# Summing the states of a selective scan by accumulating transfers, and sending token numbers instead of token rows

## The chip, the cores and the metric

One core of one Trainium2 chip. The metric is device microseconds of one execution of the whole program, all of it float32; the profile is of one further execution. PE is the matrix engine (PEld its weight loads), DVE the vector engine, ACT the scalar engine, POOL the GpSimd engine and SP the engine that issues most transfers. A queue of transfers carries the name of the engine that issues it (SPq, POOLq).

## What is computed

Three blocks with a residual each, on 16 sequences of 64 tokens of 512 numbers (1024 tokens):

```python
x = x + xattn(layernorm(x), ctx, ctx)        # 16 heads of 64: the reshape makes one row of 16 heads out of two
                                             # rows of 512, so 32 query rows and 256 key rows a sequence
x = x + ssm(layernorm(x))                    # d_inner 1024, 16 states
x = x + moe(layernorm(x))                    # 16 experts, 4 of them a token, hidden width 256

# inside ssm, for each token t of a sequence:
h = exp(dt[:, :, None] * A) * h + dt[:, :, None] * B_t * x_t[:, :, None]
y_t = einsum('bds,bs->bd', h, C_t) + D * x_t          # a sum over the 16 states s
# then y @ out_proj_w.T
```

In the mixture each token's rank over the experts gives it four slots, each expert's slots are cut in blocks of 128 rows, and the four expert outputs of a token are added with its weights.

## The kernel before

The 16 sequences go in four groups (0 to 3) of 256 tokens. A group passes attention, then projections, then the scan of its 16 states; the loop over groups runs the attention of group g+1 beside the scan of group g. Order on each engine is written out by hand and semaphores tie the engines together.

**The scan** (`scan_step`, DVE). Each state of a group is three DVE instructions over 128 x 2048: the input `u*B` into `state` (L1347), the scan itself with the decay (L1350), and the product with C (L1354) which is written over the decay buffer it has just used. ACT writes the decays, eight activations a state (L1104, `scan_decay`). There are three decay buffers (NDEC), so the decay of state j+3 may be written only when the product of state j has been read; ACT waits for that in `decay_buffer_free`. The B and C rows come broadcast from DRAM by SP into two buffers (`load_bc`, tile `bc_bcast`).

**The sum over states**, groups 0 to 2. PE adds in PSUM: `start_sum` (L673) multiplies `D*x` by the identity into four banks, and `sum_state` (L679) adds one product, four matmuls of 128x512, each of which the profile shows as two records. So a state is 8 records. They stand in PE's program between the matmuls of the next group's attention: states 0 to 2 in `attn_prep`, 3 to 11 in the eight attention units, 12 and 13 at the attention's end, 14 and 15 in `projections`. `copy_sum` brings the banks back. Group 3's states are added on DVE (L1361) beside the first experts.

**Attention.** `attn_prep(g)` makes the queries (L616), a bias of the keys (L622), and the queries carried into the context's space (L646), copied out by ACT (L959), with one decay after each of four pieces. `key_bias` (ACT, L980, eight activations) and `row_bias` (PE, L665, 16 matmuls of one column) turn the key bias into one number a row; `neg_max` on DVE (L1289, L1290) uses it. A unit then is scores (L691), exponentials, transposes (L700) and the weighted context (L712). After eight units come L743 and L751, and DVE adds the result to the residual (L1296). SP loads 1 MB of context a unit (`ctx`), and after each attention 4 MB of projection weights (`queries_ctx<-in_dt_t` first), which PE needs at L772.

**The experts.** POOL clears the table of slots in DRAM (`xd`, 20,224 rows of 2 KB), 40 transfers of up to 1 MB (L1632), one allowed after each of the attention units 8 to 15 in turns. For each group it then scatters token rows into the slots by 32 indirect transfers (`dispatch`, L1641). SP loads 128 rows a block (`load_block_x`, L453); there are 39 blocks of groups 0 to 2 and 23 of group 3 (wave 1). A block is a transpose (L801), gate and up (L811), a transpose of the hidden row (L820) and down (L832). POOL gathers outputs by 32 indirect transfers (`collect`, L1650).

## Time and profile before

| | us |
|---|---|
| three timed runs | 1369.01, 1369.88, 1376.7 (median 1369.88) |
| profiled execution, its own time | 1377.52 |
| span of its trace | 1375.8 |
| PE busy | 1176.5 (86%) |
| DVE busy | 881.7 (64%) |
| ACT busy | 631.7 (46%) |
| POOL busy | 134.1 (10%) |
| HBM read, written | 197.03 MB, 68.29 MB |

A busy share is a mean over stages with different limits. A row of the timeline has start and duration in us, then engine, line, operation, output<-input, and in brackets how long the engine was idle before it and who ended that. "128*128" of a matmul is the weight tile; a count of records of PE is twice that of its matmuls. A line number is one of the kernel before.

### The profile page before, as it was taken

What the parts mean: (1) busy time and instruction counts of PE and PEld (TensorE: products, weight loads), DVE (VectorE), ACT (ScalarE), POOL (GpSimd) and SP (SyncE); (2) the same over time, 40 slices, a digit from 0 to 9 for tenths busy, and PEclk for the clock granted to TensorE, in tenths of its full rate; (3) what the DMA queues carried; (4) which work ended last, traced back from release to release, by engine and by line L of the source; (5) the groups of instructions that cost most, each with busy time, mean ns of one, the idle gap of its engine ahead of it and who ended that gap; (6) DMA issues with size and microseconds to landing.
All of it is one profiled execution on the core that took longest, in us unless ns stands there. A gap on an engine that the chain in (4) does not pass through costs nothing.

```text
span 1375.8 us, 13572 instructions
## 1 busy us (share of the span) xinstructions
PE 1176.5 (86%) x4404; PEld 757.3 (55%) x4404; DVE 881.7 (64%) x946; ACT 631.7 (46%) x1398; POOL 134.1 (10%) x113
## 2 busy tenths in 40 slices
PE   5996869777897899999789999935999999999993
PEld 4884736555464557667456766533454445545451
DVE  1121376875657789995878998585999993323312
ACT  4452565445247466736555663642545441223221
POOL 0010001311000007000001600021000000223102
PEclk9897988999899799999889999957999998999997
DMA  7256101999630025540003523018899993999993
GB/s 272 77 169 251 40 16 43 388 401 358 213 127 8 9 70 160 150 144 15 14 10 107 168 60 140 9 61 297 317 380 358 363 374 111 371 354 408 409 397 123
DMA packets 114037, 266.22 MB, mean 194 GB/s; under 512 B 10160, under 2 KB 43056, under 8 KB 113968
## 3 DMA queue, kind: packets, MB, share of 16 engines
q1 hardware_dynamic: 98096, 207.16, 43.2%
q0 software_dynamic: 15872, 58.20, 10.8%
q8 instruction: 36, 0.59, 0.2%
q14 instruction: 33, 0.27, 0.1%
HBM read 197.03 MB, written 68.29 MB: 193 GB/s over the span
## 4 chain that ended last, share of the span: by engine, by line
PE 50%; DVE 29%; DMA 9%; ACT 8%; issue 3%; POOL 1%; SPq 0%; POOLq 0%; DVEq 0%; ACTq 0%
DVE state L1350 10%; PE bank L811 8%; PE bank L679 7%; PE bank L772 7%; PE bank L691 5%; DVE state L1347 5%; PE bank L832 4%; PE bank L712 4%; DMA ctx<-in_ctx_t 4%; DVE state L1357 2%; DVE y_acc L1361 2%; DVE decay L1354 2%; ACT decay L1104 2%; PE bank L616 2%; PE bank L646 2%
## 5 line engine op out<-in xcount | busy, mean ns | idle before, releaser
L1350 DVE TENSOR_TENSOR_SCAN state<-decay,state 128x2048 f32<-128x2048 f32 x64 | 283.0, 4421 | 40.2 <-ACT decay L1104 39.4
L811 PE MATMUL bank<-expert_w,block_x_t 128*128 128x512 f32 x496 | 227.4, 602 | 1.8 <-ACT block_x_t L1156 1.7
L679 PE MATMUL bank<-decay,params 128*128 128x512 f32 x384 | 183.5, 624 | 4.3 <-DVE decay L1354 4.3
L1104 ACT ACTIVATE decay<-delta_even,params 128x256 f32<-128x256 f32 x256 | 107.2, 496 | 103.7 <-PE bank L679 95.2
L1641 POOL DMA_INDIRECT dispatched<-ffn_x,slot x32 | 73.0, 2281 | 779.0 <-DVE slot L1443 770.5
L811 PEld LDWEIGHTS bank<-expert_w,block_x_t 128*128 128x128 f32 x496 | 91.8, 195 | 93.9 <-issue 91.9
L691 PE MATMUL bank<-ctx,queries_ctx 128*128 128x256 f32 x512 | 120.8, 392 | 19.7 <-DMA ctx<-in_ctx_t 18.5
L712 PE MATMUL bank<-probs,ctx 128*128 128x256 f32 x512 | 121.9, 393 | 11.6 <-ACT probs L1013 6.9
L1104 ACT ACTIVATE decay<-delta_odd,params 128x256 f32<-128x256 f32 x256 | 106.2, 499 | 43.6 <-PE bank L679 34.0
L679 PEld LDWEIGHTS bank<-decay,params 128*128 128x128 f32 x384 | 75.5, 200 | 84.7 <-issue 78.0
L712 PEld LDWEIGHTS bank<-probs,ctx 128*128 128x128 f32 x512 | 100.9, 198 | 36.4 <-issue 14.9
L832 PE MATMUL bank<-expert_w,hidden_t 128*128 128x512 f32 x248 | 117.0, 594 | 2.9 <-ACT hidden_t L1170 2.9
L772 PE MATMUL bank<-normed_t,queries_ctx 128*128 128x256 f32 x512 | 115.0, 385 | 4.2 <-DMA queries_ctx<-in_dt_t 3.1
L691 PEld LDWEIGHTS bank<-ctx,queries_ctx 128*128 128x128 f32 x512 | 98.5, 197 | 36.5 <-DMA ctx<-in_ctx_t 19.9
L1498 DVE SCALAR_TENSOR_TENSOR hidden<-hidden,bank 128x256 f32<-128x256 f32 x62 | 26.1, 421 | 142.2 <-ACT hidden L1160 129.0
L772 PEld LDWEIGHTS bank<-normed_t,queries_ctx 128*128 128x128 f32 x512 | 98.5, 193 | 22.9 <-issue 4.1
L1354 DVE TENSOR_TENSOR decay<-state,bc_bcast 128x2048 f32<-128x2048 f32 x48 | 109.5, 2282 | 0.8
L1347 DVE TENSOR_TENSOR state<-u_even,bc_bcast 128x2048 f32<-128x2048 f32 x32 | 73.4, 2293 | 37.4 <-DMA bc_bcast<-bc_scratch 36.6
L1160 ACT ACTIVATE hidden<-bank 128x256 f32<-128x256 f32 x62 | 23.7, 382 | 141.8 <-PE bank L811 133.4
L832 PEld LDWEIGHTS bank<-expert_w,hidden_t 128*128 128x128 f32 x248 | 46.8, 190 | 61.1 <-issue 57.4
L1166 ACT ACTIVATE block_y<-bank 128x512 f32<-128x512 f32 x62 | 37.1, 598 | 83.6 <-PE bank L832 79.0
L1347 DVE TENSOR_TENSOR state<-u_odd,bc_bcast 128x2048 f32<-128x2048 f32 x32 | 73.3, 2290 | 0.8
(196 smaller groups left out, 1398.9 us busy)
## 6 DMA issues: line engine op xcount, KB each, us to landing
dispatched<-ffn_x POOLq DMA_DIRECT2D x38, 1024.0 KB, 25.0
expert_w<-in_eg_t SPq DMA_DIRECT2D x62, 512.0 KB
expert_w<-in_eu_t SPq DMA_DIRECT2D x62, 512.0 KB
expert_w<-in_ed_t SPq DMA_DIRECT2D x62, 512.0 KB, 9.7
ctx<-in_ctx_t SPq DMA_DIRECT2D x32, 512.0 KB, 6.9
ctx<-in_ctx_n SPq DMA_DIRECT2D x32, 512.0 KB, 4.3
bc_bcast<-bc_scratch SPq DMA_DIRECT2D x64, 256.0 KB, 6.0
block_x<-dispatched SPq DMA_DIRECT2D x62, 256.0 KB
```

Of the source, the lines that this page charges most:

```text
L679: mm = pe.matmul(y_bank[c][:, :], ident, dA[(g * NS + j) % NDEC][:, c * 512:(c + 1) * 512], start=False, stop=(j == NS - 1))
L691: mm = pe.matmul(o, QT[g][:, k, c, qb * P:(qb + 1) * P], ctxT[n % 2][:, c, :], start=(c == 0), stop=(c == DC - 1))
L712: mm = pe.matmul(b[:, cc * Q:(cc + 1) * Q], ctxN[n % 2][:, j, c * P:(c + 1) * P], probT[n % 2][:, j, :], start=(j == 0), stop=(j == KC - 1))
L772: mm = pe.matmul(b[:, kk * gt:(kk + 1) * gt], w[:, c, (k + kk) * P:(k + kk + 1) * P], xT[g][:, c, :], start=(c == 0), stop=(c == DC - 1))
L811: mm = pe.matmul(o, xbT[q % 2][:, c, :], w_gu[q % NW][:, :, c, :], start=(c == 0), stop=(c == DC - 1))
L832: mm = pe.matmul(bank[4 + q % 2][:, :], hidT[q % 2][:, c, :], w_dn[q % NW][:, c, :], start=(c == 0), stop=(c == IC - 1))
L1104: ins = act.activation(dA[n % NDEC][:, k * gt:(k + 1) * gt], dlt[g][:, k, :], ACT.Exp, scale=par[:, c:c + 1])
L1166: act.activation(yb[q % NX], bank[4 + q % 2][:, :], ACT.Copy).then_inc(y_rdy, 1)
L1347: step(dve.tensor_tensor(h3, u[g], bs, ALU.mult))
L1350: dve.tensor_tensor_scan(h, dA[n % NDEC][:, 0:sw], h, 0.0, ALU.mult, ALU.add).then_inc(scan_rd, 1)
L1354: dve.tensor_tensor(hc, h3, cs, ALU.mult).then_inc(step_done, 1)
L1641: pool.indirect_dma_start(xd[WAVE_OF[c]], bass.IndirectOffsetOnAxis(slot[:, i:i + 1].bitcast(U32), 0), fx[:, t, :], None).then_inc(dispatc ...
```

## The change

Four edits.

1. **Sum by transfer.** `y_start` writes `D*x` into `sum_s`, which is the whole tile `normed` (128 x 2048). POOL issues for each of the first twelve states (`PE_FROM` = 12) of groups 0 to 2 a transfer SBUF to SBUF of 1 MB that adds the product to `sum_s`, each after the one before it has landed. PE's `start_sum` moves from `attn_prep` to the attention's end and starts from `sum_s`; PE then adds states 12 to 15. ACT waits for the transfer of state j, no longer for PE, before it writes the decay of state j+3. DVE's next norm waits until `start_sum` has read `normed`.
2. **Token numbers.** The slots in DRAM hold one int32 each. Two small transfers clear them, POOL scatters token numbers and stores normed token rows in token order. SP loads 128 numbers a block, and POOL gathers the 128 rows (62 indirect transfers). POOL's program is reordered around this.
3. **Row biases.** One activation copies the key bias; SP writes it to DRAM and reads it back spread over partitions. The eight scaled copies, 16 small matmuls and their copy are gone.
4. Waits that go with these: `proj_bc` for the B and C rows of the last group, `y_start` for its own.

```diff
+PE_FROM = NS - TAIL - PRE
...
-        out += [("query_ctx", g)] * (DC * DC // 4) + [("row_bias", g)] + [("query_ctx", g)] * (DC * DC // 4)
+        out += [("query_ctx", g)] * (DC * DC // 2)
...
+        sum_s = [nrm_[:, 0:NBK * GTS[g]] for g in range(NGR)]
...
+            def spread_key_bias(g):
+                sp.wait_ge(kb_rdy, g + 1)
+                rows = kb_dram[g].rearrange("b r u -> b (r u)")[:, 0:H // QB * GTS[g]]
+                sp.dma_start(rows.rearrange("b (h t) -> (b h) t", h=H // QB), kb[g]).then_inc(kb_out, 16)
+                sp.wait_ge(kb_out, 16 * (g + 1))
...
+                sp.dma_start(rowb_[:, g % 2 * NU * QB:g % 2 * NU * QB + NUS[g] * QB].rearrange("p (b u) -> p b u", b=QB),
+                             rows.rearrange("b (p u) -> p b u", p=P)).then_inc(rowb_in, 16)
...
-                    sp.wait_ge(xt_full, q - NX + 1)
-                sp.dma_start(xb[q % NX], xd[w][bass.DynSlice(row, P)]).then_inc(xb_in[q % NX], 16)
+                    sp.wait_ge(xb_in[q % NX], 16 * (q // NX))
+                sp.dma_start(bid[:, q % NX:q % NX + 1], ids[w][bass.DynSlice(row, P)]).then_inc(bid_in[q % NX], 16)
...
             def start_sum(g):
-                pe.wait_ge(ys_rdy, g + 1)
+                pe.wait_ge(sum_in, 16 * PE_FROM * (g + 1))
                 for c in range(NBK * GTS[g] // 512):
-                    pe.matmul(y_bank[c][:, :], ident, th_tmp[g][:, c * 512:(c + 1) * 512], start=True, stop=False)
+                    mm = pe.matmul(y_bank[c][:, :], ident, sum_s[g][:, c * 512:(c + 1) * 512], start=True, stop=False)
+                mm.then_inc(sum_read, 1)
...
                 if g > 0:
-                    for s in range(NS - TAIL - PRE, NS - PRE):
+                    start_sum(g - 1)
+                    for s in range(PE_FROM, NS - PRE):
                         sum_state(g - 1, s)
...
+                elif j < PE_FROM:
+                    act.wait_ge(sum_in, 16 * (last * PE_FROM + j + 1))
                 elif j < NS - 1:
-                    act.wait_ge(state_summed, n - NDEC + 1)
+                    act.wait_ge(state_summed, last * (NS - PE_FROM) + j - PE_FROM + 1)
...
-                pool.dma_start(v, fx_[:, 0:D].unsqueeze(1).to_broadcast([P, (end - first) // P, D])).then_inc(cleared, 16)
...
+            def add_state(g, j):
+                n = g * PE_FROM + j
+                if j == 0:
+                    pool.wait_ge(ys_rdy, g + 1)
+                pool.wait_ge(step_done, g * NS + j + 1)
+                if n:
+                    pool.wait_ge(sum_in, 16 * n)
+                pool.dma_start(sum_s[g], dA[(g * NS + j) % NDEC][:, 0:NBK * GTS[g]], accum_op=ALU.add).then_inc(sum_in, 16)
...
-                        pool.indirect_dma_start(xd[WAVE_OF[c]], bass.IndirectOffsetOnAxis(slot[:, i:i + 1].bitcast(U32), 0),
-                                                fx[:, t, :], None).then_inc(dispatched, 16)
+                    pool.indirect_dma_start(ids[WAVE_OF[c]], bass.IndirectOffsetOnAxis(slot[:, i:i + 1].bitcast(U32), 0),
+                                            token[:, t:t + 1], None).then_inc(dispatched, 16)
+            def gather_block(w, j):
...
+                pool.wait_ge(bid_in[q % NX], 16 * (q // NX + 1))
+                if q >= NX:
+                    pool.wait_ge(xt_full, q - NX + 1)
+                pool.indirect_dma_start(xb[q % NX], None, fxd[w],
+                                        bass.IndirectOffsetOnAxis(bid[:, q % NX:q % NX + 1].bitcast(U32), 0))\
+                    .then_inc(xb_in[q % NX], 16)
```

On PE, from the queries of group 1's attention to its second unit; this is the kernel before (line numbers of before):

```order
L622 MATMUL bank<-q_t,params 8x256 x4
L673 MATMUL bank<-queries_ctx,params 128x512 x4
L646 MATMUL bank<-q_t,attn_weights 128x256 x16
L665 MATMUL bank<-ones,normed 128x1 x16
L679 MATMUL bank<-decay,params 128x512 x4
L646 MATMUL bank<-q_t,attn_weights 128x256 x8
L679 MATMUL bank<-decay,params 128x512 x4
L646 MATMUL bank<-q_t,attn_weights 128x256 x8
L679 MATMUL bank<-decay,params 128x512 x4
L691 MATMUL bank<-ctx,queries_ctx 128x256 x16
L679 MATMUL bank<-decay,params 128x512 x4
```

and this the changed one (its own line numbers: L645 is L622 of before, L667 is L646, L699 is L691, L708 is L700, L720 is L712):

```order
L645 MATMUL bank<-q_t,params 8x256 x4
L667 MATMUL bank<-q_t,attn_weights 128x256 x32
L699 MATMUL bank<-ctx,queries_ctx 128x256 x16
L708 MATMUL bank<-params,probs 128x128 x4
L699 MATMUL bank<-ctx,queries_ctx 128x256 x8
L720 MATMUL bank<-probs,ctx 128x256 x8
```

The start of the sum, the row biases and every sum of a state have gone from here. At the attention's end, again on PE, the changed kernel has them as follows (L680 is L673 of before, L687 is L679, L753 is L751, L775 is L772):

```order
L745 MATMUL bank<-queries_ctx,attn_weights 64x256 x32
L753 MATMUL bank<-params,q_t 128x128 x8
L680 MATMUL bank<-normed,params 128x512 x4
L687 MATMUL bank<-decay,params 128x512 x8
L587 MATMUL bank<-params,normed 128x128 x8
L767 MATMUL bank<-normed_t,bc_weights 32x256 x4
L775 MATMUL bank<-normed_t,queries_ctx 128x256 x32
```

Before, the four matmuls of `start_sum` were not in this stretch; the others stood as here. On POOL, between the sums of group 1's states and the first gathers of wave 0, the changed kernel reads (L1655 is the accumulating transfer, L1663 the scatter of token numbers, L1645 the store of token rows, L1674 the gather of a block):

```order
L1645 DMA ffn_rows<-ffn_x 128x2x512 [waits ffn_x_ready]
L1655 DMA normed<-decay 128x2048 [waits state_added_by_dma,scan_step_done,y_started]
L1655 DMA normed<-decay 128x2048 [waits state_added_by_dma,scan_step_done] x5
L1663 DMA slot_token<-token,slot 14208x1 [waits slots_ready]
L1655 DMA normed<-decay 128x2048 [waits state_added_by_dma,scan_step_done]
...
L1663 DMA slot_token<-token,slot 14208x1 x7
L1674 DMA block_x<-ffn_rows,block_token 128x512 [waits block_token_in0,ffn_rows_written]
L1674 DMA block_x<-ffn_rows,block_token 128x512 [waits block_token_in1]
```

Every accumulating transfer is queued behind the landing of the last, and the scatters of the group before stand between them.

## Rows read from the trace of the kernel before

**Rows 1.** Chain that ended last, share of the span by engine (the page)
```profile
PE 50%; DVE 29%; DMA 9%; ACT 8%; issue 3%; POOL 1%; SPq 0%; POOLq 0%; DVEq 0%; ACTq 0%
```
**Rows 2.** Windows: us; busy PE, PEld, DVE, ACT, POOL; PEclk, DMA share, GB/s
```profile
179.00:236.00 57.00, 43.69 (x177) 27.93 (x176) 38.59 (x15) 36.34 (x85) 0.00 (x0) 0.85 0.09 19
236.00:372.00 136.00, 107.71 (x425) 75.25 (x423) 95.68 (x61) 59.11 (x149) 25.79 (x35) 0.93 0.92 346
433.00:602.00 169.00, 151.85 (x634) 104.47 (x632) 147.79 (x130) 99.22 (x240) 25.87 (x8) 0.94 0.29 83
660.00:830.00 170.00, 153.21 (x643) 106.54 (x641) 147.39 (x130) 98.80 (x239) 26.47 (x8) 0.93 0.24 73
```
**Rows 3.** Chain in order of time, attention of group 1
```profile
244.50 16.20 DMA ctx<-in_ctx_t
...
304.97 18.09 DMA ctx<-in_ctx_t
```
**Rows 4.** Timeline of DVE, scans of group 0 and group 1
```profile
224.98 4.42 DVE L1350 TENSOR_TENSOR_SCAN state<-decay,state 128x2048 f32<-128x2048 f32 x1 [8.13 <-ACT decay L1104]
...
285.55 2.29 DVE L1347 TENSOR_TENSOR state<-u_even,bc_bcast 128x2048 f32<-128x2048 f32 x1 [5.62 <-DMA bc_bcast<-bc_scratch]
...
524.63 4.42 DVE L1350 TENSOR_TENSOR_SCAN state<-decay,state 128x2048 f32<-128x2048 f32 x1
...
534.79 4.42 DVE L1350 TENSOR_TENSOR_SCAN state<-decay,state 128x2048 f32<-128x2048 f32 x1
```
**Rows 5.** Transfers: issues by line, KB each, median us to landing
```profile
dispatched<-ffn_x POOLq DMA_DIRECT2D x38, 1024.0 KB, 25.0
queries_ctx<-in_dt_t SPq DMA_DIRECT2D x4, 2048.0 KB, 8.9
attn_weights<-in_wv_t SPq DMA_DIRECT2D x1, 1024.0 KB, 10.7
```
**Rows 6.** Timeline of POOL
```profile
236.45 7.38 POOL L1632 DMA_DIRECT2D dispatched<-ffn_x  x10 [135.43 <-PE bank L691]
...
524.81 5.03 POOL L1641 DMA_INDIRECT dispatched<-ffn_x,slot  x1 [0.30 <-issue]
...
1219.72 0.99 POOL L1650 DMA_INDIRECT y_top<-expert_out,expert_out_slot  x1 [32.04 <-DMA expert_out<-block_y]
```
**Rows 7.** Timeline of PE, preparation of group 2's attention
```profile
456.23 3.70 PE L673 MATMUL bank<-queries_ctx,params 128*128 128x512 f32 x8
...
471.55 5.68 PE L665 MATMUL bank<-ones,normed 8*128 8x1 f32 x32 [3.49 <-ACT queries_ctx L959]
477.17 6.68 PE L679 MATMUL bank<-decay,params 128*128 128x512 f32 x8
...
494.80 7.11 PE L691 MATMUL bank<-ctx,queries_ctx 128*128 128x256 f32 x32
```
**Rows 8.** Timeline of ACT, the same stretch
```profile
466.65 3.30 ACT L1104 ACTIVATE decay<-delta_odd,params 128x256 f32<-128x256 f32 x8
469.84 2.06 ACT L959 ACTIVATE queries_ctx<-bank 128x512 f32<-128x512 f32 x4
...
483.88 3.30 ACT L1104 ACTIVATE decay<-delta_odd,params 128x256 f32<-128x256 f32 x8 [6.43 <-PE bank L679]
```
**Rows 9.** Timeline of PE, attention of group 0
```profile
34.63 5.66 PE L665 MATMUL bank<-ones,normed 8*128 8x1 f32 x32 [0.89 <-ACT queries_ctx L959]
...
109.84 6.02 PE L712 MATMUL bank<-probs,ctx 128*128 128x256 f32 x16 [4.69 <-DMA ctx<-in_ctx_n]
```
**Rows 10.** Timeline of PE, end of group 2's attention
```profile
602.06 1.09 PE L751 MATMUL bank<-params,q_t 128*128 128x128 f32 x8 [0.56 <-ACT q_t L1019]
602.99 7.03 PE L679 MATMUL bank<-decay,params 128*128 128x512 f32 x16
```
**Rows 11.** Timeline of all engines, first block of wave 0
```profile
940.62 2.58 SPq L453 DMA_DIRECT2D block_x<-dispatched  x3
...
943.57 1.10 PE L801 MATMUL bank<-params,block_x 128*128 128x128 f32 x4 [24.26 <-DMA block_x<-dispatched]
```

More of the change, by code:

```diff
@@ L74 @@
 ROWS = [E * c + b * P - TOPK * c for c, b in zip(CAP, BLOCKS)]
-CLEAR_ROWS = 512
-CLEARS = [(w, r, min(r + CLEAR_ROWS, ROWS[w])) for w in range(len(WAVES)) for r in range(0, ROWS[w], CLEAR_ROWS)]
-CLEAR_UNITS = range(8, 16)
 JMAX = max(CAP) // P
@@ L165, in perceiver_block @@
         nrm = nrm_[:, :].rearrange("p (n d) -> p n d", d=D)
-        sb8 = [nrm_[0:H, 0:NUS[g] * Q].rearrange("p (u h i) -> p u h i", u=NUS[g], h=H) for g in range(NGR)]
         bcT = [nrm_[0:2 * NS, 0:GTS[g]] for g in range(NGR)]
@@ L208, in perceiver_block @@
         rowb_ = sb("row_bias", 2 * NU * QB)
-        rowb = [rowb_[:, g % 2 * NU * QB:(g % 2 + 1) * NU * QB] for g in range(NGR)]
+        rowb = [rowb_[:, g % 2 * NU * QB:g % 2 * NU * QB + NUS[g] * QB].rearrange("p (b u) -> p u b", b=QB) for g in range(NGR)]
         ones8 = sb("ones", 1)
@@ L222, in perceiver_block @@
             probT = [pp_[:, 1024 + s * 512:1536 + s * 512].rearrange("p (j q) -> p j q", j=KC) for s in range(2)]
+            kb = [pp_[0:H, 0:GTS[g]] for g in range(NGR)]
             XP = 2 * GB * (T + TAPS - 1)
@@ L302, in perceiver_block @@
         yg_in = [sem(f"y_top_in{s}") for s in range(2)]
+        bid_in = [sem(f"block_token_in{s}") for s in range(NX)]
+        fx_out = sem("ffn_rows_written")
         dispatched = sem("tokens_dispatched")
@@ L722, in attention @@
                         scores(g, k + 1)
-                    if g > 0:
-                        for s in range(LEAD - 1, LEAD) if k == 0 else unit_states(g - 1, k - 1):
-                            sum_state(g - 1, s)
                     if k >= 1:
@@ L977, in key_bias @@
                 if g:
[L978 to L982 removed]
+                    act.wait_ge(kb_out, 16 * g)
+                act.activation(kb[g].rearrange("p (i u) -> p u i", u=NUS[g]), b[0:H, 0:GTS[g]].rearrange("p (u i) -> p u i", u=NUS[g]), ACT.Copy).then_inc(a_free, 1)
                 act.wait_ge(a_free, ja.n)
[L984 removed]
+                act.nop().then_inc(kb_rdy, 1)
             def exps(n):
@@ L1622, in _ @@
                 pool.iota(iota_i[:, IO_C + w * E:IO_C + (w + 1) * E], [[CAP[w], E]], base=0, channel_multiplier=0)
+            for w in range(len(WAVES)):
+                t0, n = WTILES[w][0], len(WTILES[w])
+                pool.iota(token[:, t0:t0 + n], [[P, n]], base=0, channel_multiplier=1).then_inc(tok_rdy, 1)
             pool.wait_ge(ones_rdy, 1)
@@ new lines, in dispatch @@
+            def dispatch(c, part=0, parts=1):
+                pool.wait_ge(slot_rdy, c + 1)
+                picks = [(TILE0[c] + t, k) for t in range(NTS[c]) for k in range(TOPK)]
+                for t, k in picks[part * len(picks) // parts:(part + 1) * len(picks) // parts]:
+                    i = t * TOPK + k
+                    pool.indirect_dma_start(ids[WAVE_OF[c]], bass.IndirectOffsetOnAxis(slot[:, i:i + 1].bitcast(U32), 0),
+                                            token[:, t:t + 1], None).then_inc(dispatched, 16)
@@ L1652, in collect, with blocks_written @@
                         .then_inc(yg_in[n % 2], 16)
-            for c in range(NGR):
-                dispatch(c)
-            for w in range(len(WAVES)):
-                end = BLOCK0[w] + BLOCKS[w]
+            def blocks_written(w):
                 pool.wait_ge(yslot_rdy, w + 1)
                 for s in range(NX):
-                    pool.wait_ge(yb_out[s], 16 * len(range(s, end, NX)))
-                for i, t in enumerate(WTILES[w]):
-                    collect(w * len(WTILES[0]) + i, w, t)
+                    pool.wait_ge(yb_out[s], 16 * len(range(s, BLOCK0[w] + BLOCKS[w], NX)))
+            for g in SUMMED:
+                if g:
+                    store_rows(g - 1)
+                for j in range(PE_FROM):
+                    add_state(g, j)
+                    if g and j > LEAD:
+                        dispatch(g - 1, j - LEAD - 1, PE_FROM - LEAD - 1)
+            store_rows(NGR - 2)
+            dispatch(NGR - 2)
+            for j in range(BLOCKS[0]):
+                gather_block(0, j)
+                if j == OUT_STEP + 3 + NX:
+                    store_rows(NGR - 1)
+            dispatch(NGR - 1)
+            for j in range(BLOCKS[1]):
+                gather_block(1, j)
+                if j - NX == 2:
+                    blocks_written(0)
+                for i, t in enumerate(WTILES[0]):
+                    if j - NX == max(2 * i + 1, i + 2):
+                        collect(i, 0, t)
+            blocks_written(1)
+            for i, t in enumerate(WTILES[1]):
+                collect(len(WTILES[0]) + i, 1, t)
 def kernel(**inputs):
```

97 lines of the change are left out of this document (46 added, 51 removed).

## The prediction

> **What bounds the kernel now.** I read the chain of waits first. PE has half of it, DVE 29% and transfers 9% [rows 1], so no engine is the limit throughout and each stage has to be read alone. The windows, cut at the stages, do that [rows 2]. Four things are to be seen.
>
> In the attention of group 1 (236 to 372 us) neither engine is full: DVE works 95.7 of 136 us, PE 107.7, while the transfers' share is 0.92 at 346 GB/s. In the same stretch of the next two groups (433 to 602 and 660 to 830) the share is 0.29 and 0.24, and DVE works 147.8 of 169 and 147.4 of 170 us. The chain says what is late in the first case: context loads, in pieces of 16 to 18 us [rows 3]. DVE's timeline says it again: 5.6 us of idle before a state, waiting for the B and C rows [rows 4]. The load that does this is the clearing of slots, 38 transfers of 1 MB that take 25.0 us to land [rows 5], ten of them issued at once at 236 us [rows 6].
>
> Where no clearing runs, DVE sets the pace of the units: two scans start 10.16 us apart (524.63 and 534.79) with no idle between them [rows 4]. The idle of such a group, 169 - 147.8 = 21 us and 170 - 147.4 = 23 us, lies nearly all before that. There, in the preparation of attention, PE works off the start of the sum (3.70), the row biases (5.68) and three states of the sum, the first of which took 6.68 us, and only then comes to the scores at 494.80 [rows 7]. ACT waits 6.43 us for one of those sums before a decay [rows 8]. In group 0's scan it is the same, one wait for a decay being 8.13 us [rows 4]; DVE works 38.6 of the 57 us there [rows 2].
>
> **The clearing goes.** 40 MB of writes become two small transfers. In group 0's scan the units then run at DVE's 10.16 us. Together with the preparation (next part) I let the whole stretch from 179 to 372 us shrink to DVE's work plus small waits: 38.6 + 95.7 = 134.3 us of work, and PE's end of attention, which comes about 19 us after the last product that is summed by transfer (9.6 to land, 9.4 to the end, below), ends it at 317 instead of 372. Gain 55 us. Its ceiling is 193 - 134.3 = 58.7. In group 0's attention, the first clearings delay a context load: PE is idle 4.69 us and the matmuls after it take 6.02 instead of 3.6 [rows 9]. Gain 6.
>
> **The row biases** leave PE: 5.66 us in group 0 [rows 9], where nothing else runs beside them, and some 2.5 us of ACT ahead. Gain 8. The transfer that replaces them goes to DRAM and back; the first use on DVE is over 15 us later, so I cost it at nothing. If it were late, only `neg_max` of each group's first unit would wait.
>
> **The sums leave PE** in preparation and units. For group 1's scan I laid out the stretch from 447 us again. ACT becomes its limit: four pieces of copies and a decay, 2.06 + 3.30 = 5.4 us each [rows 8], 21 us in all, and the last decay cannot start before state 2 has been added. DVE's first `neg_max` of the attention then falls at about 490 instead of 499, and a wait for the slots' positions shrinks by 2. Gain 11 to 12 in each of two groups. The units themselves gain nothing: DVE paces them.
>
> **The start of the sum moves** to the attention's end. There PE had 7.03 us of sums (states 12 and 13) after L751 [rows 10], then transposes and L764, about 3.5 us; beside it the projection weights land in 8.9 us after being issued 1.5 us later [rows 5]. So it was 10.5 against 10.4. With 3.7 us more, PE's side is 14.2. Cost 2.4 to 3.7 us a group; I take 2.4, three times.
>
> **The accumulating transfers** are the unknown. The trace has no transfer from SBUF to SBUF and none that adds. Each moves 1 MB, but reads both the product and the sum. From below: 2 MB of weights read and written land in 8.9 us [rows 5], so 1 MB without the addition is at least half, 4.5. From above: 1 MB landed in 10.7 us in a busy start, and in 25.0 us where ten stood in a queue. Reading twice makes the job like the 2 MB one, and here at most one is under way, so I take 8.9 and, with 0.74 us of POOL to issue (7.38 for ten [rows 6]), 9.6 us from product to sum. That fits under 10.16, barely. What is queued behind it: the next transfer on POOL, and on ACT the decay of three states later with the unit's normalisation behind it. For the decay itself 18 us are left, for ACT's exponentials of the next unit about 10. So at 9.6 the pace stays DVE's. The attention's end follows the landing of the twelfth by some 9.4 us (a decay of 3.3, then PE's and ACT's last steps). With p us from one landing to the next it ends at 190 + 12p + 9.4 in group 0's scan, where DVE's pace gives 317, and at 449 + 12p + 9.4 in group 1's, where it gives 590: the chain binds from p of 9.8 and 11, and from there each us costs 12 us a group. The scatters among them wait for DVE's scans, 5.03 us instead of 1 [rows 6], but only one stands between two transfers. For loads that now share the engines, and a PE clock that falls where PE is idle (PEclk is 0.93 already [rows 2]), I take off another 10 us over three groups.
>
> The Trainium skill, "Collectives: The Full Stack", section "The bandwidth ceiling: the fold count and why AG ≠ RS ≠ AR", says that a transfer that adds runs at about half the rate because it reads two sources. No row here shows one. "DMA: Bandwidth & Descriptors", section "Anatomy of one DMA", gives 2.0 us fixed plus bytes / 436 GB/s. By the two, an estimate: 2.0 + 2 x 2.4 = 6.8 us a transfer, and the chain would have 2 us more to spare than by the row of 8.9; the sum would be the same, without the 10 us taken off.
>
> **Tokens by number.** Scattering numbers takes as many instructions as rows did. A block's input now passes two transfers instead of one: SP's load of 128 numbers, then POOL's gather (1 us of issue where DVE is quiet [rows 6]). Before, SP issued the load at 940.62 and PE began at 943.57, having been idle 24.26 us, with DVE idle too [rows 11]. I take 4 us for a second hop (3 for the transfer, 1 to issue), once here and once at the first block of wave 1: 8 us, plus 1 for collects now between gathers. All other gathers have two blocks' time, 12 us, in front of them. If that cover went, each block would pay, in 62 blocks.
>
> **Sum.** 14 (group 0's attention) + 55 + 12 + 11 - 7 - 9 = 76, less 10 for contention: 66 us. The profiled execution took 1377.5, so 1311.5 for one like it; it stood 7.6 above the median of the three runs, 1369.88. Against that median I forecast 1304.
>
> **Rivals.** (a) *The transfers collide but keep up.* Accumulations, context and B/C rows meet at the end of every product, and p is 11.5 us. For: in group 0 such a collision cost 5.6 us a state [rows 4]. Against: there the queue was ten deep, and the share is now only 0.29. Price: the ends are 190 + 138 + 9.4 = 337 (35 gained) and 449 + 138 + 9.4 = 596 (6 gained, twice). 14 + 35 + 12 - 16 = 45, so 1325.
>
> (b) *The chain of additions becomes the bound, and the kernel is slower.* Place: POOL's wait for the transfer before. With p of 14 us the ends are 367 instead of 372 and 626 instead of 602, twice: 14 + 5 - 48 - 16 = -45, so 1415. It decides from 14 + (172.6 - 12p) + 2 x (143.6 - 12p) - 16 = 0, p = 12.7: there all gains are gone. For: the addition's rate is shown nowhere, and one busy 1 MB load took 10.7. Against: 8.9 for 2 MB.
>
> (c) *The gain is handed back among the experts.* Gathers issued beside DVE's scans take 5 us, the engines are near full there, and blocks slip by 1 us: 62 us, 1365. Against: two blocks of cover.
>
> **Chances.** Forecast 0.50 (1290 to 1318), (a) 0.25 (to 1355), (b) 0.18 over its whole span, (c) 0.07. About 1% is what a measurement of this kernel can tell from no change. Faster by over 1%: the first two but a tail, 0.73; within 1%: (c) and p near 12.7, 0.09; slower: 0.18. The range leaves out the best and the worst tenth: from 1284, without any slippage, to 1400, p of 13.5.
>
> **What would show it.** Right: a landing of the additions near 9 us; scans 10.2 us apart in all three groups; first scores of group 2 by 484; no context or B/C waits; no L665; POOL never the releaser of ACT's decay for long. Wrong: scans 12 us or more apart with ACT waiting for transfers of `normed`; DVE waiting for `block_x` after each block; PE's row after L751 more than 14 us long before L772.

## The result and the profile after

The changed kernel takes 1385.59 us (median of 4 runs, 1385.37 to 1390.52), the kernel before 1372.45 in the same job: ratio 1.0103, 95% interval 1.0062 to 1.0144. It is slower by 1%, where 1304 and a gain of 5% were forecast.

To see where the time went, the span is cut at five events that every version has: DVE's first addition of attention to the residual in groups 0, 1, 2 and 3 (stages 0 to 3), and PE's first gate-up matmul (stage 4); stage 5 runs from there to the end. So stage 0 holds group 0's attention, stages 1, 2 and 3 each hold the scan of one group beside the attention of the next, stage 4 leads to the first block of the experts, and stage 5 is the experts. The table is in us, from the timelines, and what each run is, stands below; e11 is not in it, since its profiled execution was a slow one.

| kernel | 0 | 1 | 2 | 3 | 4 | 5 | span | median |
|---|---|---|---|---|---|---|---|---|
| before | 126.2 | 245.8 | 230.8 | 228.8 | 114.2 | 430.0 | 1375.8 | 1371.7 |
| changed | 107.2 | 209.1 | 239.2 | 233.8 | 131.5 | 462.8 | 1383.6 | 1385.6 |
| e1 row biases alone | 113.0 | 235.2 | 221.7 | 221.3 | 113.7 | 425.4 | 1330.2 | 1336.7 |
| e2 changed, sums on PE | 107.8 | 201.9 | 225.7 | 222.1 | 128.0 | 464.4 | 1349.9 | 1349.9 |
| e3 e1, clearing paced | 114.3 | 207.0 | 227.7 | 222.7 | 113.1 | 426.9 | 1311.6 | 1312.6 |
| e4 e3 with additions | 115.6 | 250.6 | 236.0 | 237.8 | 116.6 | 429.6 | 1386.2 | 1385.5 |
| e5 copies, not additions | 107.4 | 193.8 | 220.8 | 220.9 | 131.1 | 463.8 | 1337.8 | 1340.7 |
| e6 no additions | 106.9 | 194.7 | 218.7 | 219.1 | 131.6 | 460.0 | 1331.0 | 1331.7 |
| e7 numbers of 512 B | 130.6 | 211.1 | 233.5 | 236.0 | 121.0 | 455.2 | 1387.4 | 1380.5 |
| e8 clearing in two parts | 107.8 | 215.5 | 222.8 | 220.5 | 114.6 | 426.5 | 1307.6 | 1315.1 |
| e9 every other state | 113.3 | 238.5 | 237.9 | 234.0 | 116.5 | 428.4 | 1368.6 | 1372.2 |
| e10 e9, wait later | 112.7 | 234.7 | 229.1 | 229.0 | 116.9 | 429.5 | 1351.9 | 1354.0 |

The median of before is that of the job of e1 to e4; it was 1371.3 to 1373.7 in the others. Before's profiled execution stood 4 to 8 us above its medians, the changed one's at its own, so differences of stages against before flatter a change by that much in all. The profiled execution of e1 stood 4.5 us below its median, that of e8 5.6 below and that of e7 9.9 above; the others lay within 3. The changed kernel gains 56 us in stages 0 and 1, and loses 8 and 5 in stages 2 and 3, 17 in stage 4 and 33 in stage 5.

The waits of the changed kernel (engine, line, what it waited for: us in total, times, longest) name two of its new transfers, `normed` (the accumulating one) and `block_token`:

```profile
POOL block_x L1674 <- DMA block_token<-slot_token: 246.9, 48, 19.7
POOL normed L1655 <- DMA normed<-decay: 186.1, 19, 13.2
DVE hidden L1500 <- ACT hidden L1160: 184.7, 34, 34.4
ACT decay L1104 <- DMA normed<-decay: 142.0, 28, 9.9
PE bank L804 <- DMA block_x<-ffn_rows,block_token: 55.1, 17, 39.1
```

Its chain, shares by engine, and then the largest share by line; transfers have 23% where they had 9 [rows 1]:

```profile
PE 34%; DMA 23%; issue 16%; DVE 13%; ACT 8%; POOL 6%; SPq 0%; POOLq 0%; DVEq 0%; ACTq 0%
DMA normed<-decay 14%; PE bank L775 7%; PE bank L814 4%; PE bank L720 4%; POOL block_x L1674 4%; PE bank L699 3%; DMA block_x<-ffn_rows,block_token 3%; DVE state L1352 3%; PE bank L687 3%; ACT decay L1104 2%; PE bank L745 2%; PE bank L639 2%; DMA block_token<-slot_token 2%; PE bank L835 2%; DVE decay L1356 2%
```

In the later units of group 1's scan POOL no longer waits for DVE but for the transfer before, as it does 19 times in all, and the transfers start 12.80, 12.90 and 13.01 us apart (POOL's timeline; 0.87 us is the issue):

```profile
479.52 0.88 POOL L1655 DMA_DIRECT2D normed<-decay  x1 [7.22 <-DVE decay L1356]
...
492.32 0.88 POOL L1655 DMA_DIRECT2D normed<-decay  x1 [9.84 <-DMA normed<-decay]
...
505.22 0.87 POOL L1655 DMA_DIRECT2D normed<-decay  x1 [7.21 <-DMA normed<-decay]
...
518.23 0.87 POOL L1655 DMA_DIRECT2D normed<-decay  x1 [8.91 <-DMA normed<-decay]
```

ACT follows them; its normalisation of the probabilities stands behind this wait, and PE behind that. The landing that ends ACT's wait at 491.80 was issued at 479.52, 12.3 us before:

```profile
491.80 1.70 ACT L1104 ACTIVATE decay<-delta_odd,params 128x256 f32<-128x256 f32 x4 [6.44 <-DMA normed<-decay]
493.41 0.89 ACT L994 ACTIVATE probs<-probs,row_sum 128x256 f32<-128x256 f32 x2
```

DVE's scans, 10.16 us apart before [rows 4] and still at 482.58 and 492.75, then slip to 12.91 and 12.01:

```profile
504.06 4.42 DVE L1352 TENSOR_TENSOR_SCAN state<-decay,state 128x2048 f32<-128x2048 f32 x1
516.97 4.42 DVE L1352 TENSOR_TENSOR_SCAN state<-decay,state 128x2048 f32<-128x2048 f32 x1
528.98 4.42 DVE L1352 TENSOR_TENSOR_SCAN state<-decay,state 128x2048 f32<-128x2048 f32 x1
```

### The profile page after: what moved, and what is told of

It reads as the page before. It is cut to its first block, busy times and chain, and to the rows that moved or that the text cites. A ratio compares the mean times of both kernels' runs of the same rounds, so it can differ in the third digit from the quotient of the medians.

```text
span 1383.6 us, 12881 instructions
## 1 busy us (share of the span) xinstructions
PE 1057.2 (76%) x3988; PEld 696.4 (50%) x3988; DVE 881.7 (64%) x946; ACT 620.4 (45%) x1366; POOL 219.7 (16%) x179
## 4 chain that ended last, share of the span: by engine, by line
PE 34%; DMA 23%; issue 16%; DVE 13%; ACT 8%; POOL 6%; SPq 0%; POOLq 0%; DVEq 0%; ACTq 0%
DMA normed<-decay 14%; PE bank L775 7%; PE bank L814 4%; PE bank L720 4%; POOL block_x L1674 4%; PE bank L699 3%; DMA block_x<-ffn_rows,block_token 3%; DVE state L1352 3%; PE bank L687 3%; ACT decay L1104 2%; PE bank L745 2%; PE bank L639 2%; DMA block_token<-slot_token 2%; PE bank L835 2%; DVE decay L1356 2%
## 5 line engine op out<-in xcount | busy, mean ns | idle before, releaser
L814 PE MATMUL bank<-expert_w,block_x_t 128*128 128x512 f32 x496 | 227.7, 603 | 0.1
L699 PE MATMUL bank<-ctx,queries_ctx 128*128 128x256 f32 x512 | 141.3, 440 | 13.3 <-issue 8.5
L1674 POOL DMA_INDIRECT block_x<-ffn_rows,block_token x62 | 94.7, 1527 | 302.7 <-DMA block_token<-slot_token 246.9
L720 PE MATMUL bank<-probs,ctx 128*128 128x256 f32 x512 | 124.8, 400 | 11.8 <-ACT probs L1008 11.8
L699 PEld LDWEIGHTS bank<-ctx,queries_ctx 128*128 128x128 f32 x512 | 114.2, 228 | 35.6 <-issue 10.8
L720 PEld LDWEIGHTS bank<-probs,ctx 128*128 128x128 f32 x512 | 102.5, 202 | 29.3 <-ACT probs L1008 14.2
L775 PE MATMUL bank<-normed_t,queries_ctx 128*128 128x256 f32 x512 | 113.9, 383 | 1.1 <-ACT u_even L1044 1.1
L1655 POOL DMA_DIRECT2D normed<-decay x36 | 31.0, 862 | 494.0 <-DVE decay L1356 308.0
L775 PEld LDWEIGHTS bank<-normed_t,queries_ctx 128*128 128x128 f32 x512 | 97.7, 192 | 19.4 <-issue 4.5
L708 PE MATMUL bank<-params,probs 128*128 128x128 f32 x128 | 25.4, 333 | 104.2 <-ACT queries_ctx L1001 58.1
L804 PE MATMUL bank<-params,block_x 128*128 128x128 f32 x248 | 45.0, 306 | 63.6 <-DMA block_x<-ffn_rows,block_token 55.1
```

What stands on the lines that cost most here:

```text
L699: mm = pe.matmul(o, QT[g][:, k, c, qb * P:(qb + 1) * P], ctxT[n % 2][:, c, :], start=(c == 0), stop=(c == DC - 1))
L720: mm = pe.matmul(b[:, cc * Q:(cc + 1) * Q], ctxN[n % 2][:, j, c * P:(c + 1) * P], probT[n % 2][:, j, :], start=(j == 0), stop=(j == KC - 1))
L775: mm = pe.matmul(b[:, kk * gt:(kk + 1) * gt], w[:, c, (k + kk) * P:(k + kk + 1) * P], xT[g][:, c, :], start=(c == 0), stop=(c == DC - 1))
L804: mm = pe.transpose(bank[q % 2][:, c * P:(c + 1) * P], v[:, c, :], ident)
L814: mm = pe.matmul(o, xbT[q % 2][:, c, :], w_gu[q % NW][:, :, c, :], start=(c == 0), stop=(c == DC - 1))
L1674: pool.indirect_dma_start(xb[q % NX], None, fxd[w], bass.IndirectOffsetOnAxis(bid[:, q % NX:q % NX + 1].bitcast(U32), 0))\
```

## The experiments

**The parts apart.** Four kernels tell which edit gains and which loses.

e1 is the kernel before with the row biases by transfer and nothing else of the change.

```diff
+            spread_key_bias(0)
...
-                    if c == 1:
-                        row_bias(g)
...
-                    dve.wait_ge(rowb_rdy, g + 1)
+                    dve.wait_ge(rowb_in, 16 * (g + 1))
```

> The kernel before with the row biases by transfer as the only edit. If the 5.7 us of small matmuls and the copies around them were on the path: the first add to the residual (126.2 us before) comes at 113 +- 2, and the three later preparations of attention win 3 to 6 us each, 1350 us in all. Rival (the transfer's round trip or DVE hides it): within 1% of before.

1336.73 us, ratio 0.9748 (0.9715 to 0.978): the row biases gain 35 us by the medians, more than was expected, and the rival falls. PE's timeline of group 0 shows 12 of them, the first scores at 36.09 in e1 and at 48.14 in the kernel before:

```profile
27.97 6.93 PE L670 MATMUL bank<-q_t,attn_weights 64*128 64x256 f32 x48 [0.31 <-ACT queries_ctx L971]
36.09 7.14 PE L703 MATMUL bank<-ctx,queries_ctx 128*128 128x256 f32 x32 [1.19 <-issue]
```
```profile
48.14 7.14 PE L691 MATMUL bank<-ctx,queries_ctx 128*128 128x256 f32 x32 [1.22 <-issue]
```

In the preparation of group 2's attention the same part is on the path too. In the kernel before the first scores come 31.26 us after the first products of q and the key weights (494.80 [rows 7] less the 463.54 of the first row here); in e1 it is 463.49 - 440.08 = 23.41:

```profile
463.54 2.00 PE L646 MATMUL bank<-q_t,attn_weights 64*128 64x256 f32 x16
```
```profile
440.08 2.00 PE L670 MATMUL bank<-q_t,attn_weights 64*128 64x256 f32 x16
...
463.49 7.07 PE L703 MATMUL bank<-ctx,queries_ctx 128*128 128x256 f32 x32
```

So 7.9 of the 9.1 us that stage 2 gains lie there, against 5.68 of product and 3.49 of idle ahead of it [rows 7].

e2 is the changed kernel with all sums of states on PE, as before.

```diff
-                elif j < PE_FROM:
-                    act.wait_ge(sum_in, 16 * (last * PE_FROM + j + 1))
                 elif j < NS - 1:
-                    act.wait_ge(state_summed, last * (NS - PE_FROM) + j - PE_FROM + 1)
+                    act.wait_ge(state_summed, n - NDEC + 1)
...
```

> The changed kernel with the sums over states put back on PE where they were; token numbers and row biases stay. Theory A (the accumulating transfers, 12.4 us apart, hold the scans of groups 1 and 2): those two stages go from 239 and 234 us to 225 or less, group 0's to about 200, and the kernel is 20 to 35 us faster than the changed one, 1355. Theory B (the transfer of numbers is what costs, in the expert stage): the 132 us from the last attention's end to the first gate-up and the 463 us behind it stay as they are, whatever happens to the sums. Rival to A (PE's sums cost as much as the transfers): 1385, no change.

1349.88 us, 0.983 (0.979 to 0.987). Theory A holds: the accumulating transfers cost 36 us by the medians, by the stages 7.2, 13.5 and 11.7 in stages 1 to 3. Theory B holds beside it: stages 4 and 5 stay at 128.0 and 464.4.

In the kernel before and in e1 the 40 clearings are let go five at a time, behind the attention units 8 to 15. e3 is e1 with them let go earlier and paced by the scan: 6 transfers in stage 0, 12 at the start of group 0's scan, and from there two a state.

```diff
-            for n in range(8, 16):
-                pool.wait_ge(s_full, n)
-                clear(5)
+            pool.wait_ge(kb_rdy, 1)
+            clear(6)
+            pool.wait_ge(dl_rdy, 1)
+            clear(12)
+            for j in range(LEAD, PE_FROM + 2):
+                pool.wait_ge(step_done, j)
+                clear(2)
+            clear(2)
```

> The kernel before with row biases by transfer and the 40 clearing transfers let go earlier and evenly (6 once the first loads are in, 12 at the start of group 0's scan, 2 a state after). No accumulating transfer, no token numbers. If the clearing hurts before only by its bunching: group 0's stage falls from 246 to about 205 us, the expert stages stay at 114 and 430 us, 1303 us in all. Rival (41 MB of writes cost their time wherever they stand): 1335 or more.

1312.64 us, 0.9564 (0.9525 to 0.9602), the best of the study. Stage 1 falls from 235.2 to 207.0 with every byte of the clearing still there; only 5.1 us separate it from e2, which clears nothing. (Stage 2 is 6.0 us longer than in e1.) What cost time was how the clearings met the loads, not the bytes in all: a clearing lands in 10.1 us here, in 25.0 before [rows 5]. In stage 1 of e1 (113.0 to 348.1 us), and then of e3 (114.3 to 321.3), DVE waited for B/C rows and PE for context as follows (us in total, times, longest):

```profile
DVE state L1353 <- DMA bc_bcast<-bc_scratch: 37.6, 7, 8.3
PE bank L703 <- DMA ctx<-in_ctx_t: 16.4, 5, 5.2
```
```profile
DVE state L1353 <- DMA bc_bcast<-bc_scratch: 11.5, 6, 4.3
PE bank L703 <- DMA ctx<-in_ctx_t: 2.3, 2, 2.1
```

e3 changes two things at once, the length of the queue and the number of clearings beside the units (22, where e1 has 35), and no run takes them apart.

e4 is e3 with the accumulating transfers, tokens scattered as rows; on POOL the clearings stand between the additions.

```diff
+                for j in range(PE_FROM):
+                    add_state(g, j)
+                    if g == 0:
+                        clear(3 if j < 8 else 2)
```

> The changed kernel with token rows scattered as before instead of numbers; accumulating transfers and row biases stay. The clearing transfers stand between group 0's additions, so group 0's stage is not to be compared. Theory B: the last two stages are back at 114 and 430 us, 45 to 50 us less than in the changed kernel. If scatters of numbers also slow the additions in groups 1 and 2, the additions land closer to 9 us and the stages are shorter than 239 and 234; if the additions are slow by themselves, they stay.

1385.53 us, 1.0091 (1.006 to 1.0123). Stages 4 and 5 are back at 116.6 and 429.6, 48 us less than in the changed kernel, so theory B holds: sending numbers costs that much there. With no scatter of numbers anywhere, stages 2 and 3 are still 8.3 and 15.1 us longer than in e3, so the additions are slow by themselves. Stage 1 is 43.6 longer: there clearings and additions are issued from one queue.

**What makes the additions slow.** e5 leaves the addition out of the transfers; the sums over states 0 to 11 are so left out.

```diff
-                pool.dma_start(sum_s[g], dA[(g * NS + j) % NDEC][:, 0:NBK * GTS[g]], accum_op=ALU.add).then_inc(sum_in, 16)
+                pool.dma_start(sum_s[g], dA[(g * NS + j) % NDEC][:, 0:NBK * GTS[g]]).then_inc(sum_in, 16)
```

> The changed kernel, its 36 transfers of 1 MB copying the product over the sum instead of adding it (the sums over states 0 to 11 are left out). The time from the first add to the residual in group 1 to that in group 2 (stage 2) is 239.2 us in the changed kernel and 225.7 with the sums on PE. Theory A, the addition is what takes the time: a copy lands in 5 to 6 us (additions 9.5 median), the units run at DVE's 10.2 us, stage 2 falls to 226 or less, the whole to 1350 or less. Theory B, any 1 MB from SBUF to SBUF that shares the engines with context and B/C loads takes as long: landing 8.5 us or more, stage 2 at 235 or more, the whole at 1375 or more.

1340.7 us, 0.977 (0.9754 to 0.9787). The transfers' rows in the changed kernel and in e5 (KB each, median us to landing):

```profile
normed<-decay POOLq DMA_DIRECT2D x36, 1024.0 KB, 9.5
```
```profile
normed<-decay POOLq DMA_DIRECT2D x36, 1024.0 KB, 7.2
```

7.2 is between the two figures expected, but the time decides for A: 45 us come back. In e5 POOL waits for DVE again, and the starts are 10.16 us apart, DVE's pace:

```profile
459.29 0.54 POOL L1655 DMA_DIRECT2D normed<-decay  x1 [7.26 <-DVE decay L1356]
469.46 0.54 POOL L1655 DMA_DIRECT2D normed<-decay  x1 [7.25 <-DVE decay L1356]
479.62 0.54 POOL L1655 DMA_DIRECT2D normed<-decay  x1 [7.26 <-DVE decay L1356]
```

e6 issues no such transfer, and ACT waits for the product instead; the same sums are left out.

```diff
-                    add_state(g, j)
...
-                    act.wait_ge(sum_in, 16 * (last * PE_FROM + j + 1))
+                    act.wait_ge(step_done, last * NS + j + 1)
```

> The changed kernel without the 36 accumulating transfers (sums over states 0 to 11 left out); ACT's decays wait for the product instead. Theory A, the chain product, transfer, next transfer, decay is all of the loss in the three scans (with the sums on PE stages 1 to 3 are 201.9, 225.7, 222.1): the stages fall below those by what PE no longer does, to about 195, 215 and 212, the whole to 1350 (the expert stages stay at 131 and 463). Rival, the moved start of the sum and the order at the attention's end hold the time as well: stages 2 and 3 stay at 225 or more and the whole at 1370.

1331.71 us, 0.9699 (0.9675 to 0.9723). Theory A holds within 7 us a stage: 194.7, 218.7, 219.1. It also says what the edit could have been worth at best: 7, 7 and 3 us against e2. The copies of e5 lose 2 us of that in each of stages 2 and 3.

**Additions with slack between them.** e9 is e3 with the even states 0 to 10 added by transfer and the others by PE (`BY_DMA = range(0, PE_FROM, 2)`).

```diff
+                if j in BY_DMA:
+                    return
                 pe.wait_ge(step_done, g * NS + j + 1)
```

> The kernel with paced clearing and row biases by transfer (1312.6; stages 1 to 3: 207.0, 227.7, 222.7), in which the even states 0 to 10 of a group are added by accumulating transfers and the others by TensorE, so that two units' time (over 20 us) lies between two transfers and the chain of additions cannot set the pace. Theory A, only the chain's length made the additions slow: TensorE has less to do than in that kernel, stages 1 to 3 come to about 204, 222 and 220, the whole to 1300 to 1308. Rival, an accumulating transfer also costs the context and B/C loads beside it: stages 2 and 3 stay at 227 and 222 or go above, the whole at 1313 to 1325.

1372.21 us, 1.0006 (0.9986 to 1.0025), far above both theories. Theory A falls: in stages 2 and 3 no transfer waits for the one before, and they are still 10.2 and 11.3 us above e3's. Stage 1 is 31.5 us above; there the first addition is issued behind twelve clearings, and the second waits 35.1 us for it. In stages 2 and 3 there are two reasons. One is the rival's: these waits for B/C rows and context (351.8 to 823.7 us; us in total, times, longest), of which e3 has none there:

```profile
DVE state L1362 <- DMA bc_bcast<-bc_scratch: 16.2, 6, 4.7
PE bank L706 <- DMA ctx<-in_ctx_t: 8.6, 3, 3.9
```

ACT's timeline shows the other. This landing was issued at 478.74, right behind the product, and ACT stood before its decay from 482.94, 4.2 us after that:

```profile
491.65 1.70 ACT L1117 ACTIVATE decay<-delta_odd,params 128x256 f32<-128x256 f32 x4 [8.71 <-DMA normed<-decay]
493.26 0.89 ACT L1007 ACTIVATE probs<-probs,row_sum 128x256 f32<-128x256 f32 x2
```

e10 and e11 put both halves of a unit's decay behind the normalisation, in e9 and in the changed kernel:

```diff
-                    if now:
-                        scan_decay(g - 1, now[0], 0, NBK // 2)
                     normalise(n)
...
                     if now:
-                        scan_decay(g - 1, now[0], NBK // 2)
+                        scan_decay(g - 1, now[0])
```

> The kernel of the run with every other state added by transfer (1372; stages 1 to 3: 238.5, 237.9, 234.0), in which ACT makes both halves of a unit's decay after it has normalised the unit's probabilities and kept the context, instead of the first half before. Theory A, the landing stands at the head of ACT's queue 4.5 us after the product's end and holds the normalisation, and PE, behind it: the waits for landings shrink, stages 2 and 3 fall to about 228 and 224, the whole to 1345 or less. Theory B, the transfers themselves take the engines from the context and B/C loads: stages 2 and 3 stay within 3 us, the whole at 1365 or more.

1353.95 us, 0.9865 (0.984 to 0.989). 18 us come back, and stages 2 and 3 fall by 8.8 and 5.0; B's bound of 3 us does not hold, and A's figures are not reached. The waits of ACT for landings in e9, then in e10, with the longest of each in stage 1, behind the clearings:

```profile
ACT decay L1117 <- DMA normed<-decay: 70.5, 9, 19.2
```
```profile
ACT decay L1117 <- DMA normed<-decay: 41.5, 7, 19.0
```

The order accounts for most of the loss in stage 2 (229.1 against e3's 227.7) and under half of that in stage 3 (229.0 against 222.7). In e10's stages 2 and 3 DVE still waits 7.5 us for B/C rows and PE 8.7 for context, which could account for much of the rest; no run removes those waits alone.

> The changed kernel (1385.6; stages 1 to 3: 209.1, 239.2, 233.8) with the same move of ACT's decay behind the normalisation. Theory A, each addition waits for the landing of the one before, 12 to 13 us in the stretch from 479 to 532 us, and that alone sets the pace: stages 2 and 3 stay within 3 us. Theory B, the wait's place in ACT's queue sets the pace: both fall by 8 us or more, the whole to 1365 or less.

1371.84 us, 0.9997 (0.9974 to 1.002), 14 below the changed kernel, in another job: more than A allows, less than B asks. Its profiled execution lay 13 us above that median, so its stages say nothing on which of them gained. The split between the landing's length and its place in ACT's queue stays open for the changed kernel.

**The token numbers.** e7 scatters each number as a row of 512 B (repeated 128 times); the load of 128 numbers and the gather stay.

```diff
-                                            token[:, t:t + 1], None).then_inc(dispatched, 16)
+                                            fx[:, t - TILE0[c], 0:P].bitcast(I32), None).then_inc(dispatched, 16)
```

> The changed kernel with token numbers scattered as rows of 512 B (the number repeated 128 times) in place of 4 B; the second transfer of a block's way stays. From the last attention to the first block (stage 4) and from there to the end (stage 5) the changed kernel takes 131.5 and 462.8 us, a kernel that scatters the token rows 113.1 and 426.9. Theory A, writes of 4 B hold the transfer engines: stage 4 falls to about 118, stage 5 to about 435, the whole to 1345. Theory B, the second transfer itself, queued behind the experts' weights, is what is late: stage 4 stays at 128 or more, stage 5 at 455 or more, the whole above 1370.

1380.45 us, 1.0052 (1.0035 to 1.007). The total decides nothing: clearing those rows takes 10 MB in stage 0, and the stage is 23 us longer. 18.1 of these are one wait for the row biases, whose transfer comes late beside that clearing:

```profile
DVE neg_max L1291 <- DMA row_bias<-key_bias_rows: 18.1, 1, 18.1
```

Stages 4 and 5 fall by 10.5 and 7.6, so both theories hold in part. PE's wait for the first block's tokens separates them. It is 39.07 us in the changed kernel, 26.47 in e7 and 23.80 in e3, which has no second transfer (24.26 before [rows 11]):

```profile
918.73 2.27 PE L804 MATMUL bank<-params,block_x 128*128 128x128 f32 x8 [39.07 <-DMA block_x<-ffn_rows,block_token]
```
```profile
928.09 1.10 PE L804 MATMUL bank<-params,block_x 128*128 128x128 f32 x4 [26.47 <-DMA block_x<-ffn_rows,block_token]
```
```profile
882.39 1.10 PE L813 MATMUL bank<-params,block_x 128*128 128x128 f32 x4 [23.80 <-DMA block_x<-dispatched]
```

The size of the writes costs 12.6 us there, the second transfer 2.7. At the change of waves it is alike. From the first gate-up matmul of wave 0's last block to that of wave 1's first, PE's timeline has 34.5 us in the changed kernel, 21.8 in e7 and 15.5 in e3: 12.7 for the size, 6.3 for the second transfer. In the changed kernel POOL issues eight scatters from 1163.21 to 1172.19, and SP's next load of numbers, which waits for them, starts only at 1195.74:

```profile
1172.19 0.97 POOL L1663 DMA_INDIRECT slot_token<-token,slot  x1 [0.30 <-issue]
1208.70 0.99 POOL L1674 DMA_INDIRECT block_x<-ffn_rows,block_token  x1 [35.53 <-issue]
```

Transfers of that stretch (1163 to 1216 us): the weights that pass beside the eight scatters take 18 to 22 us to land, where the medians over all 62 blocks are 6.3 to 8.6, and where the same loads take 4.2 to 5.9 in e7's like stretch (1180 to 1218 us; second fence). The window from 1175 to 1215 us (columns as in [rows 2]) has the transfer engines at 0.94 of their time with only 218 GB/s, and PE busy for 19.38 of 40 us; e3 moves 371 GB/s at a share of 1.00 from 1130 to 1155 us:

```profile
expert_w<-in_ed_t SPq DMA_DIRECT2D x6, 512.0 KB, 18.5
expert_w<-in_eg_t SPq DMA_DIRECT2D x4, 512.0 KB, 20.4
expert_w<-in_eu_t SPq DMA_DIRECT2D x4, 512.0 KB, 22.1
...
slot_token<-token,slot POOLq DMA_INDIRECT x8, 16.1
```
```profile
expert_w<-in_ed_t SPq DMA_DIRECT2D x6, 512.0 KB, 5.9
expert_w<-in_eg_t SPq DMA_DIRECT2D x4, 512.0 KB, 4.2
expert_w<-in_eu_t SPq DMA_DIRECT2D x4, 512.0 KB, 5.8
```
```profile
1175.00:1215.00 40.00, 19.38 (x46) 8.94 (x46) 1.68 (x4) 4.93 (x12) 2.92 (x3) 0.80 0.94 218
```

The rest of stage 5 is slippage of blocks: from first to last block of a wave the changed kernel takes 259.3 and 135.6 us, e3 251.0 and 126.9. That is 17 us over 62 blocks, and e7 has it too (262.9 and 137.7), so it goes with the gather by number and not with the size of the writes.

**Clearing in two parts.** e8 clears wave 1's rows only during group 1's and 2's scans, from a zero row of 512 B.

```diff
+                if g == 1:
+                    for j in range(8, 20):
+                        pool.wait_ge(step_done, NS + j)
+                        clear(1)
```

> The kernel before with the row biases by transfer, and the clearing spread further than in the run with paced clearing (1312.6): wave 0's 28 MB while group 0 is scanned, wave 1's 12 MB in the second half of group 1's scan and the start of group 2's, from a zero row of 512 B. Theory, clearing costs only where context loads queue behind it: stage 0 falls from 114.3 to 108, stage 1 stays at 205 to 209, stages 2 and 3 rise by 2 at most, the whole 1305. Rival, four times as many packets of a quarter of the size cost as much as the bunching did: stage 1 at 215 or more, the whole at 1320 or more.

1315.07 us, 0.9589 (0.9565 to 0.9614), the same as e3. Stage 0 gains the 6.5 us expected (107.8), stage 1 gives back 8.5 (215.5, the rival's side). It is not the number of clearings: 28 fall in that stage, where e3 has 34. DVE waits 17.5 us for B/C rows there (11.5 in e3) and PE 6.5 for a context load (2.3 in e3). The smaller rows are the likelier cause, but it is not shown: both profiles count 15872 packets in POOL's queue, not four times as many here, and only the issue of a clearing is longer (1.1 us against 0.7).

## Why the prediction was wrong, step by step

**The clearing goes: near in size, cause in part wrong.** Group 0's attention was to gain 6; e2 gains 5.2 on e1 in stage 0. The stretch of group 0's scan was to gain 55, with the sums free: e6, where they are, gains 51.1 in stage 1 (245.8 - 194.7), of which 10.6 are the row biases'; 40.5 are left for the clearing and the sums together. And I took it that the bytes had to go: e3 keeps them all and ends stage 1 within 5.1 us of e2.

**The row biases: mechanism right, size wrong.** 8 us were forecast for group 0 alone; it was 12 there. What failed here is that later groups would gain nothing: their preparation is a chain through PE and ACT with DVE waiting behind it. Stages 1, 2 and 3 gained 10.6, 9.1 and 7.5 us. It is 35 us by the medians instead of 8.

**The sums leave PE: overrated.** 12 and 11 us a group were given to it. e6 against e2 has 7 and 3 in stages 2 and 3. That the row biases had taken part of it is likely, but no run has the one without the other.

**The accumulating transfers: the first failed step.** I took 8.9 us from a load of 2 MB and 0.74 to issue, so p of 9.6 under DVE's 10.16, and the pace was to stay DVE's. The median landing, 9.5, is near that; what counts is the landing where it meets the context and B/C loads, and there p was 12.8 to 13.0, with POOL and ACT waiting for landings. From the first issue of a group to its last landing the trace has 133.4, 153.9 and 146.9 us, so p of 11.1, 12.8 and 12.2 for groups 0, 1 and 2, where the copies of e5 need 9.9, 11.1 and 11.0. My formula holds for the length of the stages: with these p it gives 207, 240 and 233 us, and 209.1, 239.2 and 233.8 were measured. And the "about 10" us that I left for ACT's next exponentials were too many: in e9 ACT stood before the landing 4.2 us after the transfer's issue. Together the additions lost 36 us against sums on PE (e2). I had 23 us of gain for the sums that leave PE, less 7 for the moved start and 10 for contention, so the step is off by some 42 us.

The place is that of rival (b), to which I gave 0.18. But that the total came out near its break-even, p of 12.7, is luck: with the p of the three groups the formula leaves a gain of 24 us. What made the kernel slower is the next step, which (b) left at 9 us, less what the row biases gained beyond my 8.

**Tokens by number: the second failed step, and the larger one.** 9 us were forecast for second hops; they measured 2.7 and 6.3 at the two places, so that term was right. What failed is what I put at nothing: the scatters, which I had counted only as "as many instructions as rows did", cost 12.6 and 12.7 us more by the size of their writes, and the blocks' cover of 12 us did not hold fully: 17 us of slips, a quarter of rival (c)'s price. Stages 4 and 5 against e1: 17.8 and 37.4, so 55 instead of 9. My rivals took one failure at a time, and (b) and (c) both came true in part.

By the profiled spans: before to e1, the row biases, -45.6; e1 to e2, clearing and numbers, +19.7; e2 to the changed kernel, the additions, +33.7: +7.8 together. By the medians it is -35, +13, +36: +14. The middle figure is two: e2 gains 38.5 us on e1 in stages 0 and 1, where the clearing has gone, and loses 53.3 in stages 4 and 5. So the additions lose in the scans and the numbers among the experts, and together they eat what the row biases and the missing clearing gain.

## What to carry to other kernels

A transfer that stands in for an engine's work is priced by its landing in the busiest stretch and by what is queued behind the wait for it, not by its median; and if the next one must wait for it, its landing is a pace. Count small writes by their number, not their bytes: 4 KB in 4-byte pieces held up the weights of several blocks. Before removing bulk traffic, try to spread it: issuing it earlier and in smaller groups gave 24 us, without a byte less.

## What the runs showed of the hardware

A transfer of 1 MB within SBUF landed in 7.2 us by median (e5), with the addition in 9.5; POOL's issue of one took 0.54 and 0.86 us. The addition thus takes 2.3 us more, a third. These are landings beside other loads; no run here has a lone one. The Trainium skill's "Collectives: The Full Stack", section "The bandwidth ceiling: the fold count and why AG ≠ RS ≠ AR", has reduction at half the rate of gathering, because it reads two sources. In the prediction's estimate from that page and the skill's "DMA: Bandwidth & Descriptors" the second read is 2.4 us of 6.8, so the runs agree with it in the difference; in the whole they do not, since a landing of 9.5 stands against the 6.8, and one of 7.2 against the 4.4 that the same estimate leaves for a copy.

Beside eight scatters of 128 numbers each, 4 KB in all, loads of 512 KB took 18 to 22 us to land (changed kernel); with 512 B a number, 128 times the bytes, they took 4.2 to 5.9 (e7), and the step is 12.7 us shorter. The Trainium skill, "DMA: Bandwidth & Descriptors", section "Specifications", says that writes under 512 B are done by read-modify-write; the two runs agree with it in direction.

PE's granted clock was 0.891 over the changed kernel, 0.905 in e5 and 0.937 in e2. That mean does not follow the lost time alone: e6, without a transfer to wait for, has 0.895, and there as in the changed kernel PE has less work. Locally it shows: the 16 records of L699 below took 5.05 us behind 3.55 us of idle in the changed kernel, where the granted clock was 0.71 (468.40 to 474.30 us), and 3.62 behind 1.34 us in e5, where it was 1.00 (469.10 to 473.20). So this wait for a landing cost more than its own length.

```profile
468.44 0.93 PE L708 MATMUL bank<-params,probs 128*128 128x128 f32 x4 [3.55 <-ACT queries_ctx L1001]
469.16 5.05 PE L699 MATMUL bank<-ctx,queries_ctx 128*128 128x256 f32 x16
```
```profile
469.02 0.63 PE L708 MATMUL bank<-params,probs 128*128 128x128 f32 x4 [1.34 <-ACT queries_ctx L1001]
469.48 3.62 PE L699 MATMUL bank<-ctx,queries_ctx 128*128 128x256 f32 x16
```
